# The last layer's tiles 2 to 9 turned by VectorE in 32x32 squares and put in place by sixteen small DMAs each

## The chip, the cores and the metric

The kernel runs on one core of one Trainium2 chip. The core has five engines with instruction streams of their own, which meet at semaphores: TensorE (PE, matmuls and transposes), VectorE (DVE), ScalarE (ACT), GpSimd (POOL) and SyncE (SP, which here only issues DMAs); 16 DMA engines carry the transfers. SBUF is the on-chip memory with 128 partitions, PSUM the memory that TensorE writes to, in 8 banks of 512 fp32 columns. The metric is the time of one execution in microseconds (us).

## What is computed

Four graph layers on 1250 nodes with 1024 features and 20000 edges, each with a residual. Only the fourth is touched. Cut to it:

```python
h = jnp.maximum(_layernorm(x, axis=-1), 0.0)
x = x + L3(h, W, a, src, dst)

def L3(x, W, a, src, dst):
    h = x @ W                                    # 1250x1024 @ 1024x1024
    al, ar = h @ a[0, :d], h @ a[0, d:]
    e = jnp.exp(-leaky_relu(al[src] + ar[dst], 0.1))
    rowsum = segment_sum(e, src)
    h_prime = segment_sum(e[:, None] * h[dst], src) / (rowsum[:, None] + 1e-5)
    return elu(h_prime)
```

## The kernel before

The 1250 nodes are padded to 1280: T = 10 tiles of 128 rows, in HT = 5 pairs. A product `h @ W` of fp32 accuracy is made of three products of fp32r operands: each operand is split into a high part and a rest (`hi`, `lo`), and hi*hi, hi*lo and lo*hi are summed in PSUM. For TensorE the rows of a tile must lie transposed in SBUF, as 8 blocks (k) of 128 features by 128 nodes.

The last dense layer (`dense[2]`, written d3) takes these steps for a tile t, with b = t % 2 as the number of its buffers:

- SP loads the tile of x into `xin[b]` (`load_x3`, line 861), once the transposes of tile t-2 have read that buffer.
- VectorE takes mean and variance (`stats_dve`, lines 571 to 575) and ScalarE subtracts the mean and applies the ReLU in place (`h_act`, line 618). The factor 1/deviation is applied behind the product: `root_act` and `scale_dve` (lines 585 to 593) compute it for two tiles at a time.
- TensorE transposes the tile, 8 times 128x128, from `xin[b]` into PSUM banks 6 and 7 (`transpose_pe`, line 642). That piece stands in the middle of the product of tile t-1, between its k = 3 and k = 4.
- ScalarE copies the transposed tile to `hT_hi[b]` (`transposed_act`, line 625), and VectorE subtracts that from it to get `hT_lo[b]` (`transposed_dve`, line 632).
- TensorE makes the product (`product_pe`, line 659): 8 blocks of 6 matmuls of 512 columns, into two PSUM banks. It waits for `hT_lo[b]` and for the last reading of these banks, two products before (`product_read`).
- ScalarE writes the scaled product as `y_hi` (`y_act`, line 1435), and VectorE reads the product three times: two dot products with the attention vectors (lines 2070 and 2073) and `y_lo` (line 2075), which releases the banks; then four tiny operations (`scores`).

In the product of tile 9 stands `spread_al` (line 2480), which the attention needs; VectorE and ScalarE start the attention (`attention_start`) between the scores of tile 8 and of tile 9. Its weights are multiplied by the edge counts, `count`, which SP loads in five pieces (`load_count`, line 865), each for two tiles; VectorE waits for all five in `attention_start`. The order on each engine is that of the code: `dense_pe`, `dense_dve` and `dense_act` write out a loop over the pairs, and SP's block has the order of the loads. The same three functions and the same transposes serve the second layer's product, which the change does not touch.

Of the kernel before, what the change touches and what calls it, by code (L numbers as in the profile page):

```python
# [14 lines left out]
ALU = mybir.AluOpType  # L15
ACT = mybir.ActivationFunctionType
AX_X = mybir.AxisListType.X
F32 = mybir.dt.float32
# [6 lines left out]
P = 128  # L25
D = 1024
# [4 lines left out]
T = -(-N // P)  # L31
# [56 lines left out]
RELU_UNITS = [n for n, (kind, _, _) in enumerate(UNITS) if kind in ("A12", "S4", "S3", "A22")]  # L88
W3_AT = {23: 0, 24: 1, 25: 2, 26: 3, 30: 4, 31: 5, 32: 6, 33: 7}
TRANSPOSE_UNIT = 32  # L90
W3_FREE = [(0, 0, 2 * T3 + 2), (0, 0, 2 * T1 + 2), (0, 0, 2 * T4 + 2), (22, ADD_OF["S3", 1] + 1, 0), (24, ADD_OF["S3", 3] + 1, 0),
           (28, len(ADDS), 0), (32, len(ADDS), 0), (35, len(ADDS), 0)]
EARLY = 3
# [10 lines left out]
def build_program(nc, x, src, dst, edge_weight, w1, b1, gate_w, gate_b, bias1, w2, b2, w3_dram, att, out):  # L104
# [10 lines left out]
    def at(name, shape, dtype, offset):  # L115
        return nc.alloc_sbuf_tensor_at(name, shape, dtype, offset=offset)
# [82 lines left out]
    cnt = [at(f"cnt{k}", [P, BANK], F32R, R_X + 2 * k * KIB) for k in range(COUNT_RING)]  # L199
    top = at("top", [P, BANK], F32R, R_X + 8 * KIB)  # L200
    low = at("low", [P, BANK], F32R, R_X + 10 * KIB)


    y_all = at("y_all", [P, T, 2, D], F32R, R_Y)
# [298 lines left out]
    block = ctx.enter_context(nc.Block())  # L503


    TRANSPOSED = ps[:, 6 * BANK:8 * BANK]

    PRODUCTS = [ps[:, (2 + 2 * b) * BANK:(4 + 2 * b) * BANK] for b in range(2)]
# [26 lines left out]
    def rows(t):  # L535
        return bass.ds(t * P, P)
# [58 lines left out]
    def scale_pool(pool, i):  # L595

        done = NORM_STEPS * i
        pool.wait_ge(var_ready, i + 1)
        nc.gpsimd.tensor_tensor(rough[:, :], variance[:, :], minus_half[:, :], ALU.pow).then_inc(norm_chain0, 1)
        pool.wait_ge(norm_chain0, done + 1)  # L600
        nc.gpsimd.tensor_tensor(square[:, :], rough[:, :], rough[:, :], ALU.mult).then_inc(norm_chain0, 1)
        pool.wait_ge(norm_chain0, done + 2)
        nc.gpsimd.tensor_tensor(square[:, :], square[:, :], variance[:, :], ALU.mult).then_inc(norm_chain0, 1)
        pool.wait_ge(norm_chain0, done + 3)
        nc.gpsimd.tensor_scalar(step[:, :], square[:, :], -0.5, 1.5, ALU.mult, ALU.add).then_inc(norm_chain0, 1)
        pool.wait_ge(norm_chain0, done + 4)
        nc.gpsimd.tensor_tensor(scale0[:, i, :], rough[:, :], step[:, :], ALU.mult).then_inc(scale_first, 1)
        pool.wait_ge(scale_first, i + 1)
        nc.gpsimd.tensor_tensor(bias_scale[:, i, :], scale0[:, i, :], variance[:, :], ALU.mult).then_inc(scale_ready, 1)

    def root_act(act, d, i):
        act.wait_ge(var_ready, d.norm_pairs(i) + 1)
# [2 lines left out]
    def h_act(act, d, i, b):  # L615

        act.wait_ge(shift_ready, d.tiles(2 * i + b + 1))
        nc.scalar.activation(xin[b][:, :], xin[b][:, :], ACT.Relu, bias=shift[:, b:b + 1]).then_inc(h_ready, 1)
# [77 lines left out]
    def dense_act(act, d, finish, late):  # L696

        with act.Fori(0, HT - 1) as i:
            for b in range(2):
                transposed_act(act, d, i + b, 1 - b)  # L700
                h_act(act, d, i + 1, b)
                finish(i, b)
            root_act(act, d, i + 1)
        transposed_act(act, d, HT - 1, 1)
        finish(HT - 1, 0)
        late()
        finish(HT - 1, 1)
# [52 lines left out]
    def _(sp):  # L760
# [89 lines left out]

        sp.wait_ge(unit_done, UNIT_OF["S1", PAIRS - 1] + 1)
        load_w3(0)
        def load_x3(i):
            for b in range(2):
                t = 2 * i + b
                if t < PAIRS:
                    sp.wait_ge(half_stored[t], 64)
                else:
                    sp.wait_ge(bottom_added, 16 * T)
                sp.wait_ge(h_transposed[b], d.norm_pairs(i))  # L860
                sp.dma_start(xin[b][:, :], x3_dram[rows(t), :]).then_inc(xin_landed[b], 16)

        def load_count(i):

            sp.dma_start(count[:, bass.ds(2 * i, 2), :], count_dram[bass.ds(2 * i * P, 2 * P), :].rearrange("(t p) s -> p t s", p=P)
                         ).then_inc(count_landed, 16)

        load_x3(0)
        sp.wait_ge(unit_done, UNIT_OF["S4", PAIRS - 1] + 1)
        load_w3(1)  # L870
        load_x3(1)
        sp.wait_ge(w_lo_ready, KT * 3)
        for i in range(2, HT):
            load_x3(i)
            load_count(i - 2)
        load_count(HT - 2)
        load_count(HT - 1)

        def load3(i, b):
            if i > 0:  # L880
# [176 lines left out]
    def _(act):  # L1057
# [373 lines left out]
        def y_act(d, i, b):  # L1431
            t = 2 * i + b
            act.wait_ge(product_ready[b], d.pairs(i + 1))
            act.wait_ge(scale_ready, d.norm_pairs(i) + 1)
            nc.scalar.activation(y_all[:, bass.ds(t, 1), 0, :].rearrange("p a n -> p (a n)"), PRODUCT[d.n][b], ACT.Identity,
                                 scale=scale[:, b:b + 1]).then_inc(y_hi_ready, 1)
# [67 lines left out]
            exps(0, 0)  # L1504
            attention_act(0, range(EARLY), True, False)

        dense_act(act, dense[2], lambda i, b: y_act(dense[2], i, b), attention_start)
        attention_act(0, range(EARLY, T), True, False)
        for grp in range(1, GROUPS - 1):
            attention_act(grp, range(T), False, False)  # L1510
# [15 lines left out]
    def _(dve):  # L1526
# [626 lines left out]
            att_of(0, 0)  # L2153
            attention_dve(0, range(EARLY), True, False)

        dense_dve(dve, d3, scores, attention_start)
        dve.wait_ge(al_ready, 3 * T)
        attention_dve(0, range(EARLY, T), True, False)
        for grp in range(1, GROUPS - 1):
# [21 lines left out]
    def _(pe):  # L2181
# [299 lines left out]
                                        al[:, t:t + 1].to_broadcast([P, P]), ident[:, :], start=True, stop=True)  # L2481
            last.then_inc(al_spread, 1)

        dense_pe(pe, dense[2], lambda b: pe.wait_ge(unit_read, (UNIT_OF["S4", 3] + 1, UNIT_OF["A22", 2] + 1)[b]), lambda: spread_al(range(AL_FIRST)))

        def gat_step(s, j, ns):

# [85 lines left out]
```

## Time and profile before

| | us |
|---|---|
| median of 3 runs | 974.82 (973.36 to 975.26) |
| the profiled execution | 974.37 |
| its span | 972.6 |
| TensorE busy | 955.2 (98%) |
| VectorE busy | 713.5 (73%) |
| ScalarE busy | 496.8 (51%) |
| GpSimd busy | 152.0 (16%) |

The span is what the profile shows between the first and the last instruction; the execution's own time is 1.8 us longer. A matmul's duration in the profile overlaps with the next, so the pace of TensorE is read from the starts of its instructions or from the chain of waits, not from durations. The last dense layer lies between 710 and 829 us.

### The profile page before, as it was taken

The page shows a single profiled execution, that of the slowest core. Times are in us where ns is not written, and L with a number is a line of the kernel's source. Part 1 is how long each engine was busy: PE and PEld are TensorE (multiplying, and loading weights), DVE is VectorE, ACT ScalarE, POOL GpSimd, SP SyncE. Part 2 cuts the span into 40 slices and gives each one's busy share as a digit, 9 for nine tenths or more (in the row PEclk, how much of TensorE's full clock was granted, in tenths as well). Part 3 has the DMA queues.
Part 4 walks back from the last instruction along what each step waited for, and adds up shares of the span by engine and source line. Part 5 has one row for each costly group of instructions (what it writes and reads, how often), then busy time and mean ns, then how long its engine had stood idle before and what let it go on. Part 6 is the DMA issues. An engine that isn't in the chain of part 4 may idle for free.

```text
span 972.6 us, 14172 instructions
## 1 busy us (share of the span) xinstructions
PE 955.2 (98%) x5140; PEld 794.5 (82%) x5140; DVE 713.5 (73%) x1277; ACT 496.8 (51%) x768; POOL 152.0 (16%) x197
## 2 busy tenths in 40 slices
PE   5999999999999999999999999999999999999998
PEld 3888878888888888888888888888888888888887
DVE  7987798788788789558885162797856664967787
ACT  5778864554554557323334344444622323656654
POOL 3022410000000001132223000014210000333331
PEclk9999999999999999999999999999999999999999
DMA  7256491000000005453424400044952220201222
GB/s 258 88 194 230 127 209 68 0 24 0 0 22 0 0 0 119 76 172 131 129 87 126 162 1 1 1 55 116 224 126 77 82 106 0 88 22 66 86 87 82
DMA packets 28472, 83.73 MB, mean 86 GB/s; under 512 B 4696, under 2 KB 4892, under 8 KB 28272
## 3 DMA queue, kind: packets, MB, share of 16 engines
q1 hardware_dynamic: 17536, 53.48, 16.6%
q0 software_dynamic: 10880, 29.50, 12.9%
q8 instruction: 35, 0.57, 0.3%
q14 instruction: 21, 0.17, 0.1%
HBM read 54.65 MB, written 33.57 MB: 91 GB/s over the span
## 4 chain that ended last, share of the span: by engine, by line
PE 95%; DVE 1%; ACT 1%; DMA 1%; issue 1%; POOL 1%; SPq 0%; ACTq 0%; DVEq 0%; POOLq 0%
PE ps L659 22%; PE ps L2492 13%; PE ps L2467 10%; PE ps L2384 9%; PE ps L2386 9%; PE ps L2385 9%; PE ps L2440 5%; PE ps L2436 5%; PE ps L642 3%; PE ps L2307 2%; PE ps L2308 1%; PE ps L2309 1%; PE ps L2232 1%; PE ps L2235 1%; PE ps L2276 1%; PE ps L2503 1%
## 5 line engine op out<-in xcount | busy, mean ns | idle before, releaser
L2384 PE MATMUL ps<-g_hi,mask_hi 128*128 128x512 f32 x400 | 157.7, 394 | 0.2
L2386 PE MATMUL ps<-g_hi,mask_lo 128*128 128x512 f32 x400 | 155.9, 390 | 0.0
L2385 PE MATMUL ps<-g_lo,mask_hi 128*128 128x512 f32 x400 | 155.7, 389 | 0.0
L1232 ACT ACTIVATE mask<-ps,v 128x640 f32<-128x640 f32 x80 | 63.2, 793 | 95.7 <-PE ps L2386 49.1
L2492 PE MATMUL ps<-y_all,att_hi 128*128 128x512 f32 x380 | 103.6, 392 | 0.0
L2384 PEld LDWEIGHTS ps<-g_hi,mask_hi 128*128 128x128 f32 x400 | 75.1, 188 | 19.1 <-DVE mask_lo L1762 2.3
L2386 PEld LDWEIGHTS ps<-g_hi,mask_lo 128*128 128x128 f32 x400 | 75.1, 188 | 16.0
L2385 PEld LDWEIGHTS ps<-g_lo,mask_hi 128*128 128x128 f32 x400 | 75.1, 188 | 14.8
L2467 PE MATMUL ps<-w_hi,parts 128*128 128x512 f32 x280 | 86.7, 389 | 0.0
L659 PE MATMUL ps<-w,hT_hi 128*128 128x512 f32 x320 | 86.6, 392 | 0.0
L625 ACT ACTIVATE hT_hi<-ps 128x1024 fp32r<-128x1024 f32 x30 | 30.8, 1026 | 104.7 <-PE ps L642 104.6
L2492 PEld LDWEIGHTS ps<-y_all,att_hi 128*128 128x128 f32 x380 | 70.4, 188 | 14.8 <-issue 0.4
L1757 DVE TENSOR_TENSOR mask<-mask,countT 128x640 f32<-128x640 f32 x80 | 65.4, 819 | 13.9 <-ACT mask L1232 13.9
L1237 ACT ACTIVATE mask_hi<-mask 128x640 fp32r<-128x640 f32 x80 | 58.9, 737 | 28.4 <-DVE mask L1757 27.9
L659 PEld LDWEIGHTS ps<-w,hT_hi 128*128 128x128 f32 x320 | 59.3, 188 | 11.8
L2440 PE MATMUL ps<-cnt,hs 128*128 128x512 f32 (+1 forms) x240 | 64.9, 351 | 1.6 <-issue 1.6
L1762 DVE TENSOR_TENSOR mask_lo<-mask,mask_hi 128x640 fp32r<-128x640 f32 x80 | 65.1, 818 | 1.2 <-ACT mask_hi L1237 1.2
L2436 PE MATMUL ps<-cnt,hs 128*128 128x512 f32 (+1 forms) x240 | 64.7, 351 | 0.0
L659 PE MATMUL ps<-wt_hi,hT_hi 128*128 128x512 f32 x160 | 63.3, 395 | 0.0
L659 PE MATMUL ps<-wt_lo,hT_hi 128*128 128x512 f32 x160 | 62.3, 390 | 0.0
L2467 PEld LDWEIGHTS ps<-w_hi,parts 128*128 128x128 f32 x280 | 52.6, 188 | 10.8
L2492 PE MATMUL ps<-y_all,att_lo 128*128 128x512 f32 x190 | 59.4, 390 | 0.0
(248 smaller groups left out, 1989.5 us busy)
## 6 DMA issues: line engine op xcount, KB each, us to landing
xin<-x_after SPq DMA_DIRECT2D x20, 512.0 KB, 3.4
x_after<-g POOLq DMA_DIRECT2D x20, 256.0 KB, 7.6
xres<-x_after POOLq DMA_DIRECT2D x10, 512.0 KB, 3.6
x_after<-xres POOLq DMA_DIRECT2D x10, 512.0 KB, 3.1
xin<-in_x SPq DMA_DIRECT2D x9, 512.0 KB, 3.7
x_after<-in_x SPq DMA_DIRECT2D x8, 512.0 KB
weight_rows<-weight_row POOLq DMA_DIRECT2D x8, 512.0 KB, 3.9
wt_raw<-weight_rows SPq DMA_DIRECT2D x4, 1024.0 KB, 20.5
```

The source lines that it names most:

```text
L659: last = nc.tensor.matmul(PRODUCT[d.n][b][:, half * BANK:(half + 1) * BANK], left[:, k, :], right[k][:, half * BANK:(half + 1) * BANK], st ...
L1232: nc.scalar.activation(mask[k][:, :], U_ALL, ACT.Tanh, bias=v[:, s:s + 1]).then_inc(tanh_ready, 1)
L1237: nc.scalar.activation(mask_hi[k][:, :], mask[k][:, :], ACT.Copy).then_inc(mask_hi_ready, 1)
L1757: nc.vector.tensor_tensor(mask[k][:, :], mask[k][:, :], countT[:, s, h * HALF:(h + 1) * HALF], ALU.mult).then_inc(mask_ready, 1)
L1762: nc.vector.tensor_tensor(mask_lo[k][:, :], mask[k][:, :], mask_hi[k][:, :].bitcast(F32), ALU.subtract).then_inc(mask_lo_ready, 1)
L2384: nc.tensor.matmul(SUMS[dd], mask_hi[k][:, cols], g_hi[:, s, :], start=(s == 0), stop=False)
L2385: nc.tensor.matmul(SUMS[dd], mask_hi[k][:, cols], g_lo[:, s, :], start=False, stop=False)
L2386: last = nc.tensor.matmul(SUMS[dd], mask_lo[k][:, cols], g_hi[:, s, :], start=False, stop=(s == T - 1))
L2436: nc.tensor.matmul(sums[j], hs[:, f, s, 0, j * P:(j + 1) * P], columns, start=(s == 0), stop=False)
L2440: last = nc.tensor.matmul(sums[j], hs[:, f, s, 1, j * P:(j + 1) * P], columns, start=False, stop=(s == T - 1))
L2467: last = nc.tensor.matmul(UNIT_BANK[n], left, right[:, k, :], start=(kind != "A22" and k == 0 and len(rights) == 2 and right is W2_HI[w]), ...
L2492: last = nc.tensor.matmul(AGG[j][:, n * BANK:(n + 1) * BANK], left, right[:, n * BANK:(n + 1) * BANK], start=(s == 0 and len(rights) == 2 ...
```

## The change

Tiles 2 to 9 of the last layer are no longer transposed by TensorE. VectorE transposes each 32x32 square of the tile in its place, with one instruction, from `xin` into a new buffer `squares`, with its 32-column pieces in another order (`square_dve`). In a transposed tile square (i, a), that is nodes 32i and on by features 32a and on of a block of 128 features, belongs into partition group a and node group i. As VectorE does not move data between groups of 32 partitions, SP does it with sixteen DMAs, each from 32 partitions of `squares` to 32 partitions of `turned[b]`, 256 fp32 columns (1 KB) each, 32 KB in all. ScalarE and VectorE then split `turned[b]` into `hT_hi[b]` and `hT_lo[b]` (`turned_act`, `turned_dve`). There is one `squares` and two `turned`; they lie in SBUF where the count's pieces 2 to 4 go later, so that these are loaded behind the splitting of tile 9. The loops of ScalarE and VectorE over the pairs are written out tile by tile. The new waits use old semaphores again: `squares_ready` is `w2_chain`, `turned_landed` are `dst_landed` and `src_landed`.

```diff
+SQUARE = 32
+QUARTERS = P // SQUARE
+FIRST_SQUARED = 2
...
+    squares = at("squares", [P, D], F32, R_C + 10 * KIB)
+    turned = [at(f"turned{b}", [P, D], F32, R_C + (14 + 4 * b) * KIB) for b in range(2)]
...
+    squares_ready, squares_before = w2_chain, 8
+    turned_landed, turned_before = [dst_landed, src_landed], 16
...
+    def square_dve(dve, t):
+
+        dve.wait_ge(h_ready, dense[2].tiles(t + 1))
+        if t > FIRST_SQUARED:
+            dve.wait_ge(turned_landed[(t - 1) % 2], turned_before + 16 * QUARTERS * QUARTERS * ((t - 1) // 2))
+        nc.vector.transpose(squares[:, :].rearrange("p (a k r) -> p a k r", a=QUARTERS, r=SQUARE),
+                            xin[t % 2][:, :].rearrange("p (k a c) -> p a k c", a=QUARTERS, c=SQUARE)).then_inc(squares_ready, 1)
+
+    def by_k(tile):
+
+        return tile.rearrange("p (i k r) -> p k i r", i=QUARTERS, r=SQUARE)
+
+    def turned_act(act, t):
+
+        act.wait_ge(turned_landed[t % 2], turned_before + 16 * QUARTERS * QUARTERS * (t // 2))
+        act.wait_ge(product_ready[t % 2], dense[2].pairs(t // 2))
+        nc.scalar.activation(hT_hi[t % 2][:, :, :].rearrange("p k (i r) -> p k i r", r=SQUARE), by_k(turned[t % 2][:, :]),
+                             ACT.Copy).then_inc(hT_hi_ready, 1)
+
+    def turned_dve(dve, t):
+
+        dve.wait_ge(hT_hi_ready, dense[2].tiles(t + 1))
+        nc.vector.tensor_tensor(hT_lo[t % 2][:, :, :].rearrange("p k (i r) -> p k i r", r=SQUARE), by_k(turned[t % 2][:, :]),
+                                hT_hi[t % 2][:, :, :].rearrange("p k (i r) -> p k i r", r=SQUARE).bitcast(F32),
+                                ALU.subtract).then_inc(hT_lo_ready, 1)
...
+        def load_x3(t):
...
+            if t < PAIRS:
+                sp.wait_ge(half_stored[t], 64)
+            else:
+                sp.wait_ge(bottom_added, 16 * T)
+            sp.dma_start(xin[t % 2][:, :], x3_dram[rows(t), :]).then_inc(xin_landed[t % 2], 16)
...
+        for t in range(2, 4):
+            sp.wait_ge(h_transposed[t % 2], d.norm_pairs(1))
+            load_x3(t)
+        for t in range(FIRST_SQUARED, T):
+            sp.wait_ge(squares_ready, squares_before + t - FIRST_SQUARED + 1)
+            if t >= FIRST_SQUARED + 2:
+                sp.wait_ge(hT_lo_ready, d.tiles(t - 1))
+            for a in range(QUARTERS):
+                for i in range(QUARTERS):
+                    sp.dma_start(turned[t % 2][SQUARE * a:SQUARE * (a + 1), i * QUARTER:(i + 1) * QUARTER],
+                                 squares[SQUARE * i:SQUARE * (i + 1), a * QUARTER:(a + 1) * QUARTER]).then_inc(turned_landed[t % 2], 16)
+            if t + 2 < T:
+                load_x3(t + 2)
+            if t == FIRST_SQUARED + 1:
+                sp.wait_ge(w_lo_ready, KT * 3)
+                for i in range(2):
+                    load_count(i)
+        sp.wait_ge(hT_lo_ready, d.tiles(T))
         for i in range(2, HT):
-            load_x3(i)
-            load_count(i - 2)
-        load_count(HT - 2)
-        load_count(HT - 1)
+            load_count(i)
...
-        dense_act(act, dense[2], lambda i, b: y_act(dense[2], i, b), attention_start)
+        d3 = dense[2]
+
+        h_act(act, d3, 1, 0)
+        transposed_act(act, d3, 0, 1)
+        h_act(act, d3, 1, 1)
+        root_act(act, d3, 1)
+        for t in range(1, T - 1):
+            turned_act(act, t + 1)
+            y_act(d3, (t - 1) // 2, (t - 1) % 2)
+            if t + 3 < T:
+                h_act(act, d3, (t + 3) // 2, (t + 3) % 2)
+                if t % 2 == 0:
+                    root_act(act, d3, (t + 3) // 2)
+        y_act(d3, HT - 1, 0)
+        attention_start()
+        y_act(d3, HT - 1, 1)
...
-        dense_dve(dve, d3, scores, attention_start)
+        stats_dve(dve, d3, 1, 0)
+        square_dve(dve, 2)
+        transposed_dve(dve, d3, 0, 1)
+        stats_dve(dve, d3, 1, 1)
+        variance_dve(dve, d3, 1)
+        for t in range(1, T - 1):
+            if t + 2 < T:
+                square_dve(dve, t + 2)
+            turned_dve(dve, t + 1)
+            scores((t - 1) // 2, (t - 1) % 2)
+            if t % 2 == 0:
+                scale_dve(dve, d3, t // 2)
+            if t + 3 < T:
+                stats_dve(dve, d3, (t + 3) // 2, (t + 3) % 2)
+                if t % 2 == 0:
+                    variance_dve(dve, d3, (t + 3) // 2)
+        scores(HT - 1, 0)
+        attention_start()
+        scores(HT - 1, 1)
...
-        dense_pe(pe, dense[2], lambda b: pe.wait_ge(unit_read, (UNIT_OF["S4", 3] + 1, UNIT_OF["A22", 2] + 1)[b]), lambda: spread_al(range(AL_FIRST)))
+        d3 = dense[2]
+
+        pe.wait_ge(unit_read, UNIT_OF["S4", 3] + 1)
+        product_pe(pe, d3, 0, 0, True, lambda: transpose_pe(pe, d3, 0, 1))
+        pe.wait_ge(unit_read, UNIT_OF["A22", 2] + 1)
+        product_pe(pe, d3, 0, 1, False, None)
+        with pe.Fori(1, HT - 1) as i:
+            product_pe(pe, d3, i, 0, False, None)
+            product_pe(pe, d3, i, 1, False, None)
+        product_pe(pe, d3, HT - 1, 0, False, None)
+        product_pe(pe, d3, HT - 1, 1, False, lambda: spread_al(range(AL_FIRST)))
```

On TensorE, in the loop over the pairs, around the middle of the product of the even tile. Before (line 642 is the transposes, line 659 the product):

```order
L659 MATMUL ps<-w_65,hT_lo_55 128x512 x2
L659 MATMUL ps<-w_65,hT_hi_53 128x512 x4
L659 MATMUL ps<-w_65,hT_lo_55 128x512 x2
L639 REGISTER_ALU
L642 MATMUL ps<-ident,xin_50 128x128 x8
L659 MATMUL ps<-w_65,hT_hi_53 128x512 x4
L659 MATMUL ps<-w_65,hT_lo_55 128x512 x2
```

and now (line 695 is the product):

```order
L695 MATMUL ps<-w_65,hT_lo_55 128x512 x2
L695 MATMUL ps<-w_65,hT_hi_53 128x512 x4
L695 MATMUL ps<-w_65,hT_lo_55 128x512 x2
L695 MATMUL ps<-w_65,hT_hi_53 128x512 x4
L695 MATMUL ps<-w_65,hT_lo_55 128x512 x2
```

The eight transposes of the next tile are gone from between the fourth and the fifth block of the product.

On VectorE, from the statistics of an odd tile in the loop (`xin_50`, `hT_lo_56` are buffers of odd tiles, `hT_lo_55` is the even one) into the scores. Before:

```order
L571 BN_STATS stats_236<-xin_50 128x6 x2
L755 ISA
L573 BN_AGGR mv<-stats_236 128x2
L574 REGISTER_ALU
L575 TENSOR_SCALAR shift<-mv 128x1
L632 TENSOR_TENSOR hT_lo_55<-ps,hT_hi_53 128x1024
L579 TENSOR_SCALAR variance<-mv 128x2
L2069 REGISTER_ALU
L2070 ISA row_all,al_col_266<-ps,att_all_133 128x1024
L2070 ISA al_col_266 128x1
L2072 ISA
L2073 ISA row_all,al_col_266<-ps,att_all_134 128x1024
```

and now (lines 581 to 589 are the statistics, 643 is `turned_dve`, 2134 to 2139 the scores):

```order
L581 BN_STATS stats_239<-xin_50 128x6 x2
L583 BN_AGGR mv<-stats_239 128x2
L585 TENSOR_SCALAR shift<-mv 128x1
L589 TENSOR_SCALAR variance<-mv 128x2
L626 STREAM_TRANSPOSE squares<-xin_50 128x1024
L643 TENSOR_TENSOR hT_lo_55<-turned_133,hT_hi_53 128x1024
L2134 ISA row_all,al_col_268<-ps,att_all_136 128x1024
L2134 ISA al_col_268 128x1
L2137 ISA row_all,al_col_268<-ps,att_all_137 128x1024
L2137 ISA al_col_268 128x1
L2139 SCALAR_TENSOR_TENSOR y_all<-ps,scale,y_all 128x1024
```

The operation `STREAM_TRANSPOSE` stands between the statistics of a tile and the `hT_lo` of the tile before it, and the scores follow behind both.

On SP, the loads of the last layer from tile 4 on, with the semaphores they wait for. Before:

```order
L861 DMA xin_49<-x_after 128x1024 [waits h_transposed0,half_stored4,w_lo_ready]
L861 DMA xin_50<-x_after 128x1024 [waits h_transposed1,bottom_added]
L865 DMA count<-count_rows 128x2x1280
L861 DMA xin_49<-x_after 128x1024 [waits h_transposed0,bottom_added]
L861 DMA xin_50<-x_after 128x1024 [waits h_transposed1,bottom_added]
L865 DMA count<-count_rows 128x2x1280
L861 DMA xin_49<-x_after 128x1024 [waits h_transposed0,bottom_added]
L861 DMA xin_50<-x_after 128x1024 [waits h_transposed1,bottom_added]
```

and now, from the load of tile 4 on (`turned_133` is for even tiles, `turned_134` for odd ones):

```order
L895 DMA xin_49<-x_after 128x1024 [waits half_stored4]
L916 DMA turned_134<-squares 32x256 [waits w2_chain]
L916 DMA turned_134<-squares 32x256 x15
L895 DMA xin_50<-x_after 128x1024 [waits bottom_added]
L899 DMA count<-count_rows 128x2x1280 [waits w_lo_ready]
L899 DMA count<-count_rows 128x2x1280
L916 DMA turned_133<-squares 32x256 [waits hT_lo_ready,w2_chain]
L916 DMA turned_133<-squares 32x256 x15
L895 DMA xin_49<-x_after 128x1024 [waits bottom_added]
L916 DMA turned_134<-squares 32x256 [waits hT_lo_ready,w2_chain]
```

Sixteen issues now stand ahead of each load of x, and the count's pieces stand two behind the issues of tile 3 and three behind those of tile 9.

## Rows read from the trace of the kernel before

**Rows 1.** The page's chain of waits: share of the span by engine.

```profile
PE 95%; DVE 1%; ACT 1%; DMA 1%; issue 1%; POOL 1%; SPq 0%; ACTq 0%; DVEq 0%; POOLq 0%
```

**Rows 2.** The chain in order of time: start us, us, engine, tile, line, count.

```profile
715.80 0.88 PE ps L642 x8
716.68 10.93 PE ps L659 x48
727.61 0.87 PE ps L642 x8
728.48 10.90 PE ps L659 x48
...
810.12 0.87 PE ps L642 x8
811.00 10.92 PE ps L659 x48
```

**Rows 3.** Busy us by stretch: PE, PEld, DVE, ACT, POOL, clock, DMA, GB/s.

```profile
733.80:745.60 11.80, 11.80 (x58) 9.83 (x57) 7.82 (x19) 3.38 (x4) 0.00 (x0) 1.00 0.29 100
```

**Rows 4.** VectorE's timeline: start us, us, engine, line, operation, count [idle before].

```profile
714.13 0.15 DVE L575 TENSOR_SCALAR shift<-mv 128x1 f32<-128x1 f32 x1
...
723.46 1.23 DVE L2070 CUSTOM_DVE_ANT_0 row_all<-ps,att_all 128x1024 f32<-128x1024 f32 x1 [4.47 <-ACT y_all L1435]
...
735.23 1.23 DVE L2070 CUSTOM_DVE_ANT_0 row_all<-ps,att_all 128x1024 f32<-128x1024 f32 x1 [4.35 <-ACT y_all L1435]
...
737.64 1.28 DVE L2075 SCALAR_TENSOR_TENSOR y_all<-ps,scale,y_all 128x1024 f32 x1
...
741.40 1.29 DVE L571 BATCH_NORM_STATS2 stats<-xin 128x6 f32<-128x512 f32 x2 [0.25 <-issue]
...
743.18 1.22 DVE L632 TENSOR_TENSOR hT_lo<-ps,hT_hi 128x1024 fp32r<-128x1024 f32 x1
...
825.50 0.88 DVE L2087 SCALAR_TENSOR_TENSOR att_e<-al_all,v,att_e 128x256 f32<-128x256 f32 x2 [3.35 <-ACT att_e L1450]
```

**Rows 5.** ScalarE's timeline.

```profile
729.68 1.15 ACT L618 ACTIVATE xin<-xin,shift 128x1024 f32<-128x1024 f32 x1
...
740.29 1.03 ACT L625 ACTIVATE hT_hi<-ps 128x1024 fp32r<-128x1024 f32 x1 [5.01 <-PE ps L642]
743.26 1.15 ACT L618 ACTIVATE xin<-xin,shift 128x1024 f32<-128x1024 f32 x1 [1.94 <-DVE shift L575]
```

**Rows 6.** SP's timeline, and line 772: ns min/median/max.

```profile
0.79 0.41 SPq L761 DMA_DIRECT2D xin<-in_x  x1
...
3.64 0.45 SPq L772 DMA_DIRECT2D w_raw<-in_L_gnn_W  x1
...
716.76 0.34 SPq L861 DMA_DIRECT2D xin<-x_after  x1
...
787.87 1.45 SPq L865 DMA_DIRECT2D count<-count_rows  x3
...
L772 SPq DMA_DIRECT2D w_raw<-in_L_gnn_W x4: 445/698/2516, 3.6 to 7.2; - x4
```

**Rows 7.** DMA issues with median us to landing; below them line 865.

```profile
xin<-x_after SPq DMA_DIRECT2D x20, 512.0 KB, 3.4
...
count_rows<-count_row POOLq DMA_DIRECT2D x10, 320.0 KB, 2.6
...
L865 SPq DMA_DIRECT2D count<-count_rows x5: 428/430/470, 740.7 to 788.8; - x5
...
DMA to landing us min/median/max: 4.6/4.8/7.7
```

**Rows 8.** Single operations: duration ns min/median/max, first and last start, forms.

```profile
L2169 DVE TENSOR_SCALAR xres<-xres x1: 419/419/419, 968.0 to 968.0; 128x512 f32<-128x512 f32 x1
...
L992 POOL TENSOR_TENSOR xres<-xres,row_all x10: 2398/2410/3299, 420.3 to 523.5; 128x1024 f32<-128x1024 f32 x10
...
L563 DVE TENSOR_TENSOR w<-w_raw,w x8: 1212/1217/1219, 680.8 to 708.4; 128x1024 fp32r<-128x1024 f32 x8
```

More of the change, by code:

```diff
@@ L852, in _ @@
         load_w3(0)
[L853 to L861, printed above, removed]
+        def load_x3(t):
[4 more added lines that the diff above has]
+            sp.dma_start(xin[t % 2][:, :], x3_dram[rows(t), :]).then_inc(xin_landed[t % 2], 16)
         def load_count(i):
@@ L866, in load_count @@
                          ).then_inc(count_landed, 16)
-        load_x3(0)
+        for t in range(2):
+            sp.wait_ge(h_transposed[t], d.norm_pairs(0))
+            load_x3(t)
         sp.wait_ge(unit_done, UNIT_OF["S4", PAIRS - 1] + 1)
         load_w3(1)
-        load_x3(1)
-        sp.wait_ge(w_lo_ready, KT * 3)
+        for t in range(2, 4):
+            sp.wait_ge(h_transposed[t % 2], d.norm_pairs(1))
+            load_x3(t)
+        for t in range(FIRST_SQUARED, T):
[13 more added lines that the diff above has]
+        sp.wait_ge(hT_lo_ready, d.tiles(T))
         for i in range(2, HT):
-            load_x3(i)
-            load_count(i - 2)
-        load_count(HT - 2)
-        load_count(HT - 1)
+            load_count(i)
         def load3(i, b):
```

## The prediction

> **What bounds the kernel now.** I read the shares of the chain that ended last first: TensorE has 95% of it [rows 1]. So time is won only by taking work out of TensorE's stream or by closing its holes. Then the same chain in order of time, over the last dense layer [rows 2]: a pattern of 48 product matmuls in 10.90 to 10.93 us and 8 transposes in 0.87 us, nine times for tiles 1 to 9, without a hole. The table by stretches says the same: in one tile's 11.80 us TensorE is busy for 11.80 at a granted clock of 1.00, VectorE for 7.82, ScalarE for 3.38, and the DMA engines for 0.29 of it [rows 3]. VectorE is thus the second engine by far, and SP, which issues the DMAs, almost idle. Last, the timelines of VectorE and ScalarE, for the length of each step of a tile [rows 4, 5], and SP's issues with their landing times [rows 6, 7], because the change builds a new loop from these parts.
>
> **What the change removes.** Eight groups of transposes, for tiles 2 to 9, leave TensorE's stream. Each is 0.87 us on the chain: 8 x 0.87 = 6.98 us. Nothing else covers them, since they stand between matmuls that follow back to back. Tiles 0 and 1 keep theirs. On ScalarE and VectorE the two steps that read the transposed tile stay (1.03 and 1.22 us), now from SBUF instead of PSUM; a SBUF source costs VectorE 1.217 us in this kernel [rows 8], so nothing changes there. The stretched reading in runs of 32 elements has no row; I take it at nothing, and 0.3 us each at worst.
>
> **What it adds, per tile.** One VectorE transpose of 128x1024, sixteen DMA issues on SP, and their landing. All of it lies beside TensorE, as long as the loop they form is no longer than a product's 10.9 us.
>
> The VectorE transpose has no row. Two elements per clock, as in the 128x512 row of 0.419 us, would be 0.84 us; the far end is GpSimd's 2.41 us for 128x1024 [rows 8]. I take 1.2 us, the length of every ordinary VectorE operation on 128x1024 here. The Trainium skill (VectorE: DVE Perf Modes, "The three transpose paths") gives 311 ns for a 128x128 bf16 transpose on VectorE and 390 on TensorE. By it and one element per clock at 0.96 GHz, an estimate for 1024 columns is 1.24 us; its TensorE figure is not what this trace has, where eight cost 0.87 us in the stream.
>
> An issue on SP: seven in a row at the start of the kernel begin 0.475 us apart, (3.64 - 0.79) / 6; three count loads lie 0.51 apart, (1.45 - 0.43) / 2; one that stood alone took 0.34 [rows 6]. I take 0.37 for the first after a wait and 0.475 for the others. From the first issue to the start of the sixteenth is then 0.37 + 14 x 0.475 = 7.0 us. Bounds: 5.1 (all at 0.34) and 7.5.
>
> Landing, from the start of the last issue: 2.6 us for 320 KB and 3.4 for 512 KB [rows 7]. A straight line through the two gives 1.4 us at 32 KB, the far side is 3.4 (no gain from being small). I take 2.2, a little under the nearest row.
>
> **The loop.** VectorE's transpose of tile t+3 writes the same buffer that the sixteen DMAs of tile t+2 read, so it waits for them to land. One round is 1.2 + 7.0 + 2.2 and 0.1 for semaphores: 10.5 us. This is one of two rounds that compete. The other is VectorE's own order, which now is: transpose, hT_lo, scores, (scale in every second tile), statistics, then a wait for ScalarE's ReLU of the very same tile before the next transpose. From the start of scores to the end of that ReLU the trace has 730.83 - 723.46 = 7.4 us without scale and 744.41 - 735.23 = 9.2 with it [rows 4, 5], of which 0.25 is the head of a loop that unrolled code doesn't have. With 1.2 for the transpose and 1.2 for hT_lo this makes 9.8 and 11.3 us. So rounds take the longer of 10.5 and 9.8, then the longer of 10.5 and 11.3: mean 10.9 us, just the length of a product. That is the tightest place of the change.
>
> How much slack there is at its start: the shift of tile 2 is ready at 714.28 [rows 4], ReLU 1.15, transpose 1.2: 716.7. SP has just issued tile 3's load at 716.76 [rows 6], so the sixteen run from 717.1 and the last lands at 717.1 + 7.0 + 2.2 = 726.3. Product 2 would start when products 0 and 1 are done: 716.68 + 5.46 + 10.9 = 733.0 [rows 2]. It needs two things. hT_lo of tile 2, after the transpose of tile 3: 726.4 + 1.2 + 1.2 = 728.8, four us early. And the PSUM banks of product 0, which are free when the third operation of its scores is done. These scores stand behind hT_lo on VectorE, and take 3.65 us to there (735.23 to 738.9): 732.5, only 0.5 us early. So what comes late first is not the tile but the reading of the product two before it. With rounds of 10.9 against 10.9, this 0.5 stays about constant; single rounds of 11.3 eat most of it. I put 0.4 us of stall over the whole layer.
>
> **Other edits.** The loads of x for tile t+2 now stand behind the sixteen issues of tile t. They go out near 724 for tile 4 and land 3.4 us later, 5 us before its statistics start (733): hidden. If VectorE were faster they would be the next wait. Three of five count loads move behind hT_lo of tile 9, as their place in SBUF holds the new buffers. Three land at most 7.7 us after their issue [rows 7]; hT_lo of tile 9 comes 4 us before product 9 starts, and the first reader is VectorE's attention start, which in the trace begins its logits at 825.50, 9 us after product 9 started [rows 4]. Five us of cover; with the cover gone it would be a wait on VectorE in front of TensorE's attention steps. The unrolled code of three engines costs nothing that I can price. Behind the layer everything keeps its distance to product 9, so the gain is carried to the end, where TensorE still has the chain.
>
> **The sum.** -6.98 + 0.4 = -6.6 us against the profiled execution's 974.37 (span 972.6): 967.8. The median of the runs shown is 974.82, 0.45 more, so the time I expect is 968.2 us.
>
> **Rivals.**
> (a) Landing late. If sixteen small transfers land only after 3.4 us, a round is 1.2 + 7.0 + 3.4 + 0.1 = 11.7; all rounds are then bound by it, 0.8 us over a product. Seven rounds make 5.6, and the first landing is 1.2 later against 0.5 of slack: 0.7 more. 6.98 - 6.3 leaves 0.7 us of gain: 974.1. Midway (2.8 us) a round is 11.1: 2.5 to 3 us of stall, 971. For it: no row has so many transfers in flight. Against it: DMA engines are 0.29 busy [rows 3], the added 512 KB per tile is what an x load moves.
> (b) Slower: VectorE's transpose at half the rate. At 2.4 us, the rounds are 12.5 with scale and 11.7 without: mean 12.1, 1.2 over a product. Seven rounds give 8.4, the start 0.7: 9.1 against 6.98, so +2.1 us: 976.9. It decides from 2.05 us for the operation upward. For it: the operation reads in squares and no row shows its rate. Against: all other 128x1024 operations on VectorE take 1.2.
> (c) SP's queue fills. One issue of four weight loads took 2.516 us at the start, where many transfers were outstanding [rows 6]. If one of sixteen does that, a round is 12.5 and the time 974.8 + 8 x 1.6 - 7.0 = 980.6. Against it: those were 512 KB each, here a whole tile is that much. The Trainium skill speaks for this rival: DMA: Bandwidth & Descriptors, "Rules for kernel authors", says to coalesce small transfers, under 64 KB being mostly overhead; ours are 32 KB. By its fixed 2.0 us per DMA ("Anatomy of one DMA"), an estimate for sixteen that didn't overlap is 32 us per tile; the seven issues 0.475 apart say that they do overlap.
> (d) The transposes' place in TensorE's stream wasn't worth 0.87, so no change. Rows 2 speak against it: 48 matmuls take the same 10.9 with and without scale beside them.
>
> **Chances.** Forecast, 967.3 to 970: 0.52. (a), 970 to 974: 0.20, of which 0.02 falls within 0.2%. (b) 0.13 and (c) 0.10, of which 0.03 in all within 0.2% or faster. (d) 0.05, mostly within 0.2%. A measurement of this kernel can tell 0.2%, 1.9 us, from no change. Faster by more: 0.52 + 0.18 + 0.01 = 0.71; within: 0.02 + 0.02 + 0.04 = 0.08; slower: 0.21. The range goes from 966.9 (all hidden, a shade more given back) to 977, which takes in (b).
>
> **What would show it.** In the profile after: no transposes between 722 and 811 on TensorE, and products every 10.9 us. The VectorE transpose at 1.2 us. SP busy with issues for 7 to 7.5 us of each tile. VectorE's wait before each transpose in turn on the DMA and on ScalarE's ReLU, hardly one for y. If products lie 11.3 us or more apart, the wait in front of them tells which: TensorE waiting for VectorE's y_lo means the round is too long. Long issues on SP mean (c), a transpose over 2 us means (b). The forecast is wrong if TensorE's holes in the layer sum to over 2 us.

## The result and the profile after

| | before | after |
|---|---|---|
| median, us | 975.04 (973.36 to 976.10, 4 runs) | 984.52 (981.72 to 986.85, 4 runs) |
| the profiled execution, us | 974.37 | 986.85 |
| its span, us | 972.6 | 985.1 |

The changed kernel is slower: its time is 1.0099 times that of before, 95% interval 1.0072 to 1.0126. The prediction was 968.2 us, in a range of 966.9 to 977.0.

The page's chain of waits, to be read against [rows 1]:

```profile
PE 84%; SPq 7%; DVE 3%; DMA 2%; ACT 1%; issue 1%; POOL 1%; DVEq 0%; ACTq 0%; POOLq 0%
```

SPq is SP's queue, the engine that does nothing but issue DMAs. It had nothing of the chain before; now it has more than VectorE. The same chain in order of time (start us, us, what), over one round and at the end of the layer:

```profile
729.06 2.44 DMA turned<-squares
731.60 1.26 DVE squares L626
733.42 0.59 SPq L916
...
742.30 1.87 DMA turned<-squares
744.27 1.26 DVE squares L626
...
819.20 1.87 DMA turned<-squares
821.09 1.07 ACT hT_hi L637
822.19 1.03 DVE hT_lo L643
823.33 1.22 DVE row_all L2134
824.59 1.23 DVE row_all L2137
825.83 1.21 DVE y_all L2139
827.17 7.33 PE ps L695 x24
```

Where [rows 2] had TensorE alone, the chain now runs round the loop that the prediction described: transpose, sixteen issues, landing, transpose. It touches TensorE again only at product 9. SP's timeline (start us, us, line, operation, count) gives the length of the issues:

```profile
732.87 10.02 SPq L916 DMA_DIRECT2D turned<-squares  x16
742.93 0.58 SPq L895 DMA_DIRECT2D xin<-x_after  x1
```

Sixteen issues take 10.02 us, so they stand (10.02 - 0.59) / 15 = 0.629 us apart. In [rows 6] seven loads stood 0.475 apart. The tile's own view (ns min/median/max, first and last start) has all of them alike, and the two other new steps as well:

```profile
L916 SPq DMA_DIRECT2D turned<-squares x128: 507/591/1307, 719.5 to 819.2; - x128
L626 DVE STREAM_TRANSPOSE squares<-xin x8: 1245/1246/1246, 717.8 to 807.8; 128x1024 f32<-128x1024 f32 x8
...
DMA to landing us min/median/max: 1.7/1.9/5.2
```

VectorE's timeline shows the round. The piece in brackets is the idle time before, and who ended it:

```profile
731.60 1.25 DVE L626 STREAM_TRANSPOSE squares<-xin 128x1024 f32<-128x1024 f32 x1 [3.55 <-DMA turned<-squares]
...
807.79 1.25 DVE L626 STREAM_TRANSPOSE squares<-xin 128x1024 f32<-128x1024 f32 x1 [2.79 <-DMA turned<-squares]
```

Six rounds from 731.60 to 807.79 make 12.70 us each: 1.25 for the transpose, 9.45 to the start of the sixteenth issue, 1.87 from there to the landing, 0.13 between them. A product takes 10.9. Before each of the last seven transposes VectorE was idle for 2.79 us or more, and the DMAs ended that wait, so it was never its own order that set the pace. The waits of both engines over the layer (us in total, times, longest):

```profile
PE ps L695 <- DVE y_all L2139: 11.9, 7, 2.1
```
```profile
DVE squares L626 <- DMA turned<-squares: 25.1, 7, 4.3
```

TensorE waits for VectorE's `y_lo` before seven of its products, never for hT_lo. VectorE waits for the DMAs. The one wait of TensorE that is longer than its neighbours, 2.13 us before product 9 against 1.39 to 1.62 before products 4 to 8, follows the only round with an issue of 1.31 us in it.

The account, against [rows 2]. Product 0 starts at 710.36 before and at 712.80 after; product 9 at 811.00 + 5.46 = 816.46 and at 827.17. So this stretch grew by 8.3 us: 6.98 of transposes gone, 2.1 us of wait before product 2, and seven steps from 737.62 to 827.17, which at 12.79 each instead of 10.91 add 13.2 us. Then 24 matmuls of product 9 took 7.33 us instead of 5.45: 1.9 more. The stretches show the granted clock (the third number from the end):

```profile
722.00:737.00 15.00, 13.48 (x60) 10.84 (x58) 7.09 (x12) 3.31 (x4) 0.00 (x0) 1.00 0.41 125
737.50:750.20 12.70, 12.58 (x48) 10.06 (x48) 8.03 (x17) 3.22 (x3) 0.00 (x0) 0.87 0.57 182
...
814.00:826.00 12.00, 11.04 (x48) 8.80 (x48) 4.04 (x8) 2.07 (x2) 0.00 (x0) 1.00 0.23 56
827.00:842.00 15.00, 14.83 (x66) 12.40 (x67) 9.24 (x27) 7.79 (x15) 1.20 (x2) 0.89 0.21 84
```

The clock fell in products 2 and 9, both after a wait of 2.13 us, and in none of the five after one of 1.39 to 1.62. In TensorE's timeline four matmuls take 1.91 us there, and 1.07 at full pace:

```profile
737.62 1.21 PE L695 MATMUL ps<-w,hT_hi 128*128 128x512 f32 x4 [2.13 <-DVE y_all L2139]
...
739.14 1.91 PE L695 MATMUL ps<-w,hT_hi 128*128 128x512 f32 x4
```

In product 2 this only filled what would have been a wait before product 3; in product 9 it lies on the path. The layer is longer by 8.3 + 1.9 = 10.1 us. What follows it is as long as before (143.3 us). The other 2.4 us of the spans' difference came ahead of the layer, in code that the change does not touch: most of it (1.8 us) in one stretch, 540 to 550 us, where the granted clock was 0.83 instead of 1.00. The kept traces with a mean granted clock of 0.998 have this dip and those with 1.000 do not, and the executions of before come with both, so it is no effect of the change. The falls in the layer are not in every execution either. One after execution has a mean clock of 1.000, which leaves no room for any of the three. It took 981.72 us, 7.4 more than the profiled execution of before at the same clock. So the loop alone makes the kernel slower, and the clock adds to that where it falls.

### The profile page after: what moved, and what is told of

The parts are those of the page before. It is cut to its first block, busy times and chain, and to the rows that moved or that the text cites. A ratio compares the mean times of both kernels' runs of the same rounds, so it can differ in the third digit from the quotient of the medians.

```text
span 985.1 us, 14033 instructions
## 1 busy us (share of the span) xinstructions
PE 955.4 (97%) x5075; PEld 791.5 (80%) x5076; DVE 722.4 (73%) x1285; ACT 496.5 (50%) x768; POOL 154.6 (16%) x197
## 4 chain that ended last, share of the span: by engine, by line
PE 84%; SPq 7%; DVE 3%; DMA 2%; ACT 1%; issue 1%; POOL 1%; DVEq 0%; ACTq 0%; POOLq 0%
PE ps L2584 13%; PE ps L695 13%; PE ps L2549 10%; PE ps L2466 9%; PE ps L2468 9%; PE ps L2467 9%; SPq L916 7%; PE ps L2522 5%; PE ps L2518 5%; PE ps L678 2%; PE ps L2389 2%; DMA turned<-squares 2%; PE ps L2391 1%; PE ps L2390 1%; DVE squares L626 1%
## 5 line engine op out<-in xcount | busy, mean ns | idle before, releaser
L695 PE MATMUL ps<-w,hT_hi 128*128 128x512 f32 x320 | 89.1, 401 | 11.9 <-DVE y_all L2139 11.9
L654 ACT ACTIVATE xin<-xin,shift 128x1024 f32<-128x1024 f32 x30 | 34.5, 1148 | 66.9 <-DVE shift L585 66.9
L2549 PEld LDWEIGHTS ps<-w_hi,parts 128*128 128x128 f32 x280 | 52.6, 188 | 10.9
```

What stands on the lines that cost most here:

```text
L695: last = nc.tensor.matmul(PRODUCT[d.n][b][:, half * BANK:(half + 1) * BANK], left[:, k, :], right[k][:, half * BANK:(half + 1) * BANK], st ...
L2549: last = nc.tensor.matmul(UNIT_BANK[n], left, right[:, k, :], start=(kind != "A22" and k == 0 and len(rights) == 2 and right is W2_HI[w]), ...
```

## The experiments

Theory A: each issue of a DMA from SBUF to SBUF holds SP for 0.63 us, and the round of 12.7 us that sixteen of them make is what TensorE waits for. Rivals: VectorE's own order (B), the bytes or the shortness of the transfers (C), a resource that all such transfers share, whoever issues them (D). Unless said otherwise, a time stands beside 975.11 us for before (971.71 to 976.80, 13 runs) on the same chip.

### Without the DMAs

```diff
-        if t > FIRST_SQUARED:
-            dve.wait_ge(turned_landed[(t - 1) % 2], ...)
-        nc.vector.transpose(squares[:, :].rearrange(
+        if t >= FIRST_SQUARED + 2:
+            dve.wait_ge(hT_lo_ready, dense[2].tiles(t - 1))
+        nc.vector.transpose(turned[t % 2][:, :].rearrange(
...
-        act.wait_ge(turned_landed[t % 2], ...)
+        act.wait_ge(squares_ready, squares_before + t - FIRST_SQUARED + 1)
...
-            for a in range(QUARTERS):
-                for i in range(QUARTERS):
-                    sp.dma_start(turned[t % 2][...], squares[...])
```

> VectorE's 32x32 transpose writes straight into turned[b], and the sixteen DMAs are left out, so the squares are not put in their places and the last layer's product is of rows in a wrong order; all else as in the changed kernel. Theory A (the round is too long because SP needs 0.63 us for each of sixteen issues): without them only VectorE's order is left, 9.8 and 11.4 us in turn, mean 10.6, below a product's 10.9. Products follow each other 10.9 us apart, the full 7.0 us of the removed transposes show: 968 us. Theory B (VectorE's order with its wait for ScalarE's ReLU is the bound, and the DMA wait only stands where another wait would): products stay 12 us or more apart, 982 us or more.

968.43 us (967.72 to 969.16, 4 runs), 0.9935 times before (0.9912 to 0.9959). TensorE has no wait in the layer, and VectorE's in front of the transpose is:

```profile
DVE turned L626 <- ACT xin L654: 9.5, 8, 1.2
```

That is 1.2 us each for the ReLU of the same tile. So the transposes' place in TensorE's stream is worth its 7 us, and B falls: all of VectorE's new work fits beside the products.

### Four issues for the same bytes

```diff
             for a in range(QUARTERS):
-                for i in range(QUARTERS):
-                    sp.dma_start(turned[t % 2][...256 columns...], squares[...]).then_inc(turned_landed[t % 2], 16)
+                sp.dma_start(turned[t % 2][SQUARE * a:SQUARE * (a + 1), :],
+                             squares[SQUARE * a:SQUARE * (a + 1), :]).then_inc(turned_landed[t % 2], 64)
```

> Four DMAs of 32 partitions x 1024 columns (128 KB) instead of sixteen of 32x256: the same bytes, a quarter of the issues; the squares land in wrong places, so the last layer's product is not the reference's. Theory A (count of issues): four issues take 2.5 us instead of 10.1, a round's DMA part is 1.25 + 1.9 + 2 to 3 for landing = 6 us, products 10.9 us apart, 968 us. Theory C (bytes, or the landing of 512 KB within SBUF): the round keeps over 11 us, time above 978.

967.79 us (967.63 to 970.00, 4 runs), 0.9935 (0.9909 to 0.9961). SP's timeline, and the tile's view:

```profile
728.88 2.43 SPq L915 DMA_DIRECT2D turned<-squares  x4
...
L915 SPq DMA_DIRECT2D turned<-squares x32: 521/591/968, 717.2 to 792.4; - x32
```

Four issues in 2.43 us are (2.43 - 0.59) / 3 = 0.61 apart, though each moves four times the bytes. TensorE's only wait in the layer is one of 0.5 us. The number of issues counts, not their size: C falls.

### The same sixteen, read from HBM

```diff
-                                 squares[SQUARE * i:SQUARE * (i + 1), a * QUARTER:(a + 1) * QUARTER])
+                                 x2_dram[SQUARE * i:SQUARE * (i + 1), a * QUARTER:(a + 1) * QUARTER])
```

> The sixteen DMAs of a tile read the same shapes (32 rows x 256 columns) from the HBM tensor of x instead of from squares; what lands in turned is then not the turned tile, and the output is not the reference's. It measures the distance of two issues on SP. If 0.63 us belongs to DMAs from SBUF to SBUF, issues lie 0.475 us apart as at the start of the kernel, a round is 1.25 + 7.1 + 2.5 = 10.9 us, 970 us. If it belongs to many short issues in a row, whatever their source, they stay 0.63 apart and the time stays at 982 to 986 us.

970.31 us in the one execution, span 967.8, and no wait of TensorE in the layer:

```profile
740.95 7.29 SPq L916 DMA_DIRECT2D turned<-x_after  x16
...
L916 SPq DMA_DIRECT2D turned<-x_after x128: 302/421/1212, 719.7 to 800.7; - x128
```

(7.29 - 0.42) / 15 = 0.458 us apart, where the same shapes out of SBUF have 0.629. The bursts of sixteen are not all alike, but the two kinds do not overlap: 7.3 to 8.1 us here, 10.0 to 10.7 in the changed kernel. So the prediction's price of an issue was right for a source in HBM, and sixteen such issues would have been hidden. It is the source in SBUF that makes them 0.17 us longer; why it does, no run here shows.

### Two buffers for the squares

```diff
-    squares = at("squares", [P, D], F32, R_C + 10 * KIB)
+    squares = [at(f"squares{b}", [P, D], F32, place) for b, place in enumerate((R_C + 10 * KIB, R_Y + 72 * KIB))]
...
-            dve.wait_ge(turned_landed[(t - 1) % 2], ...)
+            dve.wait_ge(turned_landed[t % 2], ...)     # the DMAs of tile t-2
```

> squares gets a second buffer (for odd tiles, where y of tile 9 goes later), so that the transpose of tile t+1 no longer waits for the landing of tile t; the sixteen issues stay. Theory A: SP alone then sets the pace, 16 x 0.63 + 0.63 for the load of x = 10.7 us a tile, just under a product. The first landing stays late (2.3 us of wait before product 2). Products 10.9 us apart from there: 975.0 - 7.0 + 2.3 = 970 to 972 us. Theory B: no change, 984 us. If SP's pace with its waits is over 10.9 us, each 0.1 us costs 0.7.

977.73 us (975.15 to 979.93, 10 runs), 1.0029 (1.0013 to 1.0045). It wins 7 us on the changed kernel, less than expected, and stays above before. SP's timeline, then VectorE's waits:

```profile
743.48 10.02 SPq L920 DMA_DIRECT2D turned<-squares  x16
753.54 0.58 SPq L899 DMA_DIRECT2D xin<-x_after  x1
755.28 10.02 SPq L920 DMA_DIRECT2D turned<-squares  x16
```
```profile
DVE hT_lo L647 <- ACT hT_hi L641: 17.5, 6, 7.6
DVE squares L630 <- ACT xin L658: 9.4, 8, 1.2
```

The issues themselves are as long as before, 10.0 us for the sixteen and 0.6 for the x load in a step of 11.7. They don't follow each other closely. The chain in order of time shows what comes between:

```profile
764.71 1.87 DMA turned<-squares
766.61 1.07 ACT hT_hi L641
767.70 1.03 DVE hT_lo L647
...
777.55 1.26 DVE squares L630
...
788.24 1.92 DMA turned<-squares
```

VectorE, which works in order, stands at `hT_lo` until that tile has landed. Then come the scores, the statistics of the tile two further on, ScalarE's ReLU of it, and only then its transpose and its sixteen issues. From landing to landing that is 23.5 us for two tiles, 11.8 for one. So the second buffer removes one link of the loop, and the order on VectorE puts a looser one in its place. The expectation had SP alone as the bound.

### Two queues

```diff
-            for a in range(QUARTERS):           # SP
+            for a in range(0, 2):               # SP: eight DMAs
...
+        def half_act(t):                        # ScalarE: the other eight, behind y of tile t-3
+            act.wait_ge(squares_ready, squares_before + t - FIRST_SQUARED + 1)
+            ...
+            for a in range(2, 4):
+                for i in range(QUARTERS):
+                    act.dma_start(turned[t % 2][...], squares[...]).then_inc(turned_landed[t % 2], 16)
```

> The changed kernel with the sixteen DMAs of a tile split: SP issues the eight for partition groups 0 and 1, ScalarE the eight for groups 2 and 3, behind y of tile t-1. Theory A (each issue from SBUF to SBUF holds the issuing engine for 0.63 us): SP and ScalarE each need 5.0 us, side by side; a round's DMA part is 1.25 + 0.9 (ScalarE's start) + 5.0 + 1.9 = 9.1 us, VectorE's order with 9.8 and 11.4 in turn (mean 10.6) is under a product's 10.9: products 10.9 us apart, 968 to 969 us, ScalarE's 5 us a tile hidden as it has over 7 idle. Theory D (the 0.63 us is a resource that both queues share): the last issue still comes 10 us after the transpose, 983 to 985 us.

968.38 us (966.53 to 970.76, 6 runs), 0.9929 (0.9911 to 0.9946), beside 975.99 for before (973.40 to 977.46, 13 runs). It computes the whole result and beats both kernels. The queues' timelines, and the page's chain:

```profile
738.39 4.97 SPq L916 DMA_DIRECT2D turned<-squares  x8
...
738.40 5.28 ACTq L1566 DMA_DIRECT2D turned<-squares  x8
...
PE 95%; DVE 1%; ACT 1%; issue 1%; DMA 1%; POOL 1%; SPq 0%; ACTq 0%; DVEq 0%; POOLq 0%
```

Two queues issue at the same time. SP keeps the pace that it has alone, (4.97 - 0.59) / 7 = 0.626 us; ScalarE's is (5.28 - 0.62) / 7 = 0.67, and no run has it alone. D falls. TensorE does not wait in the layer, and the chain is that of [rows 1] again. The Trainium skill (DMA: Bandwidth & Descriptors, "Issuing engines are not separate DMA queues") says that issuing from several engines saves only the sequencer's time for the issue, usually small beside the transfer. This trace agrees with the first half. It shows that the saving, 10.0 us made 5.3, can be all that matters where many small transfers stand in a loop.

### Through HBM

```diff
-            dve.wait_ge(turned_landed[(t - 1) % 2], ...)     # VectorE, before the next transpose
+            dve.wait_ge(ew_landed, 16 + 16 * (t - 2))
...
+            sp.dma_start(square_dram[t % 2][:, :], squares[:, :]).then_inc(ew_landed, 16)
+            sp.wait_ge(ew_landed, 16 + 16 * (t - 1))
             for a in range(QUARTERS):
-                for i in range(QUARTERS):
-                    sp.dma_start(turned[t % 2][...], squares[...])
+                sp.dma_start(turned[t % 2][SQUARE * a:SQUARE * (a + 1), :].rearrange("c (i x) -> c i x", i=QUARTERS),
+                             square_dram[t % 2].rearrange("(i c) (a x) -> a c i x", c=SQUARE, a=QUARTERS)[a])
```

> Five DMAs a tile instead of sixteen: squares is stored to HBM by one DMA of 128 rows of 4 KB, SP waits for its landing, then four DMAs (one for each group of 32 partitions of turned) read it back, each 32 x 4 pieces of 1 KB. The transpose of the next tile waits for the store alone. Theory A: 1.25 + 0.35 + 3.1 for the store, which is all that the round holds (4.7 us); the tile is there at 4.7 + 4 x 0.46 + 3.2 = 10 us after its transpose began, which delays no product since it repeats every 10.9; VectorE's order sets 10.6: 968 to 969 us. Theory C (it is the bytes moved that count, and they double here): slower than the changed kernel, over 985 us.

970.45 us (967.27 to 973.85, 9 runs), 0.9952 (0.9933 to 0.9970). Also whole, and also faster than both. In SP's timeline the store goes out at 740.32 and the four loads from 743.49, then:

```profile
740.32 0.34 SPq L915 DMA_DIRECT2D square_rows<-squares  x1
743.49 1.78 SPq L918 DMA_DIRECT2D turned<-square_rows  x4
```
```profile
PE ps L696 <- DVE y_all L2141: 2.6, 1, 2.6
```

Five issues and two landings in a row are shorter than sixteen issues and one. One wait of 2.6 us for `y_lo` is left at the layer's start, which the version with two queues does not have: there the first store took 6.9 us to land, where the median is 2.7. The expectation of 968 to 969 us did not have it. That the issues alone set the time between the changed kernel and this one is not shown by it, since here the landing of the store is in the loop too.

### Fourteen and twelve on SP

The same code with another split: SP issues the first 14 (or 12) of the sixteen, ScalarE the rest. These times stand beside 975.28 us for before (973.82 to 976.69, 13 runs).

```diff
-            for a in range(0, 2):
-                for i in range(QUARTERS):
+            for a, i in [(a, i) for a in range(QUARTERS) for i in range(QUARTERS)][:14]:     # or [:12]
```

> SP issues fourteen of the sixteen DMAs of a tile, ScalarE the other two; nothing else differs from the changed kernel, and the output is whole. If the round is squares, issues one after another on SP and landing, each issue less shortens it by 0.629 us: 12.70 - 2 x 0.63 = 11.44 us. Products then start 11.44 us apart (10.9 is a product itself), product 2 is late by 2.3 - 1.3 = 1.0 us, and the sum is -7.0 + 1.0 + 7 x 0.54 = -2.2 us: 972.9, with waits of about 0.5 us on TensorE, none long enough for its clock to fall. If the sixteen cost something as a set (a resource that fills at sixteen, or any sharing with a second queue already taking it away), the time is that of the even split, 968.4; if two queues help only when balanced, it stays near 984.

975.75 us (973.60 to 976.55, 10 runs), 1.0001 (0.9990 to 1.0012).

> SP issues twelve of the sixteen DMAs of a tile, ScalarE the other four; the output is whole. By 0.629 us an issue the round is 12.70 - 4 x 0.63 = 10.18 us, shorter than a product, and VectorE's own order (10.6 us on the mean) and the product (10.9) bound the layer: no waits on TensorE but perhaps one short one, 968.2 us, and a twelfth SP issue less buys nothing more (the even split has 968.4). If an issue cost more than its distance in the trace shows, so that twelve were still too long, TensorE would wait for y_lo in each product, and the time lie between 970 and 978.

969.32 us (966.39 to 969.52, 4 runs), 0.9933 (0.9910 to 0.9955). VectorE's transposes and SP's issues with fourteen, then SP's with twelve:

```profile
730.66 1.25 DVE L626 STREAM_TRANSPOSE squares<-xin 128x1024 f32<-128x1024 f32 x1 [2.38 <-DMA turned<-squares]
...
799.24 1.25 DVE L626 STREAM_TRANSPOSE squares<-xin 128x1024 f32<-128x1024 f32 x1 [1.52 <-DMA turned<-squares]
...
743.34 8.76 SPq L916 DMA_DIRECT2D turned<-squares  x14
```
```profile
740.66 7.52 SPq L916 DMA_DIRECT2D turned<-squares  x12
```

The round with fourteen is (799.24 - 730.66) / 6 = 11.43 us, as theory A had it (11.44), and twelve are hidden but for one wait of 0.7 us before product 2. The time with fourteen is 2.8 us over the expected. In its trace product 2 waits 1.82 us, not 1.0, and its clock falls afterwards; the products up to the ninth then stand 11.54 us apart, not 11.44. That is 0.8 + 0.7 us. From product 0 to the end of product 9 its layer is only 0.6 us shorter than that of before. The remaining 1.3 us are not in the layer, and the comparison with before is uncertain by 1.1 us, so they stay unexplained.

Product 2 was no earlier because the first round took 13.5 us (717.17 to 730.66) where the others have 11.43. The chain in order of time, in the first round and at the end of the second, shows the difference:

```profile
718.52 0.34 SPq L895
...
727.19 3.37 DMA turned<-squares
...
740.09 1.87 DMA turned<-squares
```

In the first round a load of x goes out ahead of the fourteen, which costs 0.4 us, and the last of them lands after 3.37 us instead of 1.87. In the changed kernel's first round this landing took 2.44. Two issues less saved 1.24 us there and the later landing took 0.93 of it back: 2.13 - 0.31 = 1.82. Why the first landings are late is not separated by any run. The size of the round follows 0.63 us an issue; the sum over the layer was 1.5 us too low.

## Why the prediction was wrong

- **What bounds the kernel, and the 6.98 us of transposes.** Right. Without the DMAs the whole gain is there, -6.7 us.
- **VectorE's transpose at 1.2 us**, with rival (b) at 2.4: 1.246. Right.
- **Landing at 2.2 us**, with rival (a) at 3.4: 1.9 at the median, a little better, though the first round's took 2.44. (a) did not happen.
- **The issue at 0.475 us, the sixteenth starting after 7.0 us, bounds 5.1 and 7.5.** This is the step that failed. It took 9.4 us, outside both bounds. All rows behind the bounds ([rows 6]) were of issues whose source lies in HBM; in a SBUF to SBUF copy each holds the queue for 0.629 us. The experiment with an HBM source measured 0.458, so the arithmetic was right for the wrong kind of transfer. The trace of before had no row of the right kind, and the bound from above should have been left further out: the longest row at hand, 2.5 us once in four, was used only for rival (c).
- **The round of 10.5 us, "just the length of a product".** With 9.4 for 7.0 it is 12.7, 1.8 us over a product, and comes up seven times: 13.2 us. The prediction named the place as the tightest of the change. Past that point each 0.1 us per issue costs 1.5 us a round, 10.5 us over seven.
- **What comes late first: the reading of product t-2, with 0.5 us of slack at the start.** Right: all seven waits are for `y_lo`, the sign that the prediction had named for a round that is too long. In the first round the sixteenth issue started 9.5 us after the first instead of 7.0, and landed after 2.44 instead of 2.2: 2.5 and 0.2 us more, less the slack of 0.5, make 2.2 us for product 2; it was 2.13.
- **The edits costed at nothing** (the stretched reading, loads of x and of the count). Right: 1.06 and 1.18 us for the two readers of `turned`, no wait for the count, one wait of 4.7 us of VectorE for x beside waits for the DMAs that were there anyway.
- **Rival (c), SP too slow**, had the right engine and the sign, 980.6 us. Its mechanism was another: one long issue in sixteen on a full queue. It was every issue that was longer. The longest of 128 took 1.31 us; it stood in the last round and made the step from product 8 to 9 13.28 us, 0.5 more than the longest of the other steps. Beside this rival stood the Trainium skill (DMA: Bandwidth & Descriptors, "Rules for kernel authors") with its advice to coalesce small transfers. With 128 KB instead of 32 the distance stayed at 0.61, so the cost here goes by the issue. The estimate of 32 us beside it took a figure that the page of the Trainium skill gives for DMAs issued by GpSimd, and SP issued these.
- **Not foreseen:** TensorE's clock falling after its waits. In the profiled execution 1.9 us of it stood on the path, in product 9.

With the measured issues and landings put in, the prediction's own sum gives -6.98 + 2.2 + 7 x 1.8 = +7.8 us. The trace has 8.3 to the start of product 9, and the 1.9 of the clock behind it. So the mechanism that was forecast, a loop beside TensorE that must be no longer than a product, is the one that ran; one term of it was mis-sized, and that turned the gain of 6.6 us into a loss.

## What to carry over

Price a DMA issue from a row with the same source and destination, and where none exists leave the upper bound wide, above all when the count is multiplied by sixteen and stands in a loop that was found to be just as long as the work that hides it. Moving work off the busiest engine pays only while the loop that replaces it is shorter than a step of that engine; here sixteen issues on one queue gave +9.5 us, and the same sixteen on two queues -7.6. When a loop is too long, look for what is serial in it: one more buffer did not cure it, fewer issues in a row did, with the same bytes and even with the detour through HBM.

## What the runs showed of the hardware

- An issue of a DMA from SBUF to SBUF stands 0.61 to 0.63 us before the next on the same queue, with 32 KB or 128 KB alike (0.68 in the slowest burst). From HBM to SBUF in the same shapes it is 0.46 to 0.51. The issue right behind such a burst is longer too: x loads, which come from HBM, took 0.58 us there, and 0.42 behind the burst from HBM.
- SP and ScalarE issue side by side, 8 in 4.97 and 8 in 5.28 us, and SP is not slowed by it.
- A transpose of 128x1024 fp32 in squares of 32x32 takes VectorE 1.246 us, as much as its other operations on that shape.
- TensorE's granted clock fell to its lower level (1.2 GHz, four matmuls in 1.9 us instead of 1.07) for some 3 us behind waits of 1.82, 1.91, 2.13, 2.13 and 2.54 us in three kernels, and in this layer never behind one of 1.62 or less. In the stretch at 540 us it fell in the seven traces where TensorE had been idle for 1.68 to 2.06 us, and not in the three with 1.50 to 1.66. But it need not fall: in the version through HBM it stayed up behind a wait of 2.64 us. What decides, no run here shows. The first three stretches are of the kernel with two buffers for the squares, behind waits of 2.54, 1.52 and 1.91 us; the fourth is of the one through HBM:

```profile
738.00:748.00 10.00, 9.67 (x35) 7.81 (x36) 7.40 (x16) 3.21 (x3) 0.00 (x0) 0.83 0.59 198
796.00:806.00 10.00, 9.75 (x43) 8.13 (x44) 7.90 (x22) 3.20 (x4) 0.00 (x0) 1.00 0.14 36
820.00:832.00 12.00, 11.70 (x53) 9.81 (x54) 6.46 (x21) 5.08 (x8) 0.00 (x0) 0.86 0.27 105
```
```profile
735.40:748.00 12.60, 12.51 (x55) 10.38 (x56) 10.28 (x27) 3.10 (x3) 0.00 (x0) 1.00 0.72 241
```
